# A macaron block on one core: first weights loaded in 112 and 15 rows, and the steps of norms, recurrence and routing placed further apart

## The reference

```
x = x + 0.5 * moe(norm(x))      # 8 experts, 128 -> 512 -> 128, relu, the best 2 gates of a softmax
x = x + rwkv(norm(x))           # time mixing, a recurrence over the tokens, output projection
x = x + 0.5 * moe(norm(x))
x = x + 0.5 * quant_ffn(norm(x))   # int weights, 128 -> 384 -> 128
x = x + attention(norm(x))      # 16 heads of 64, rms norm, all 2048 tokens with each other
x = x + 0.5 * quant_ffn(norm(x))
```

## Time and profile before

| | |
|---|---|
| median of 3 runs | 2288.65 us (2284.3 to 2289.0) |
| profiled execution | 2287.96 us |
| its span, first to last instruction | 2286.2 us |
| mean granted TensorE clock | 0.975 |
| busy in the span | TensorE 87%, VectorE 78%, ScalarE 64%, GpSimd 68% |
| first split product of the first stage | 179.91 us |
| last y_gated of that stage | 633.1 us |

### The profile page before, as it was taken

The page is one execution under the profiler, slowest core; times in us unless marked ns, Lnnn a source line. Parts: engine busy times, 40 slices in busy tenths (PEclk is TensorE's granted clock), DMA queues, the critical chain, the costliest instruction groups (busy, mean ns, idle before and its releaser), DMA issues. The chain is left out here.

```text
span 2286.2 us, 25543 instructions
## 1 busy us (share of the span) xinstructions
PE 1996.4 (87%) x8290; PEld 1421.5 (62%) x8290; DVE 1782.5 (78%) x1964; ACT 1457.9 (64%) x1800; POOL 1543.3 (68%) x767
## 2 busy tenths in 40 slices
PE   1007998899986899999999999999999999999877
PEld 1005776667855576676676766667667667666544
DVE  0005778877655789989989988989998998999785
ACT  0005555554442578877878877878787887887753
POOL 0004233322230589989999998999998998999872
PEclk9999999999987899999999999999999999999987
DMA  1112110112004012312303213123032131230000
GB/s 41 43 47 54 47 33 25 32 38 50 26 14 114 0 40 46 66 20 63 73 13 70 50 36 66 32 52 73 15 69 45 41 67 27 54 71 16 5 1 19
DMA packets 78758, 96.76 MB, mean 42 GB/s; under 512 B 31875, under 2 KB 35379, under 8 KB 78248
## 3 DMA queue, kind: packets, MB, share of 16 engines
q1 hardware_dynamic: 78630, 95.13, 18.2%
HBM read 43.18 MB, written 1.42 MB: 20 GB/s over the span
## 5 line engine op out<-in xcount | busy, mean ns | idle before, releaser
L598 POOL TENSOR_TENSOR p_l<-p_raw,p_h 128x1024 fp32r<-128x1024 f32 x512 | 1240.9, 2452 | 146.0 <-ACT p_h L1246 130.7
L1243 ACT ACTIVATE p_raw<-ps 128x1024 f32<-128x1024 f32 x512 | 566.8, 1107 | 243.1 <-PE ps L870 242.2
L1570 DVE TENSOR_REDUCE m_part<-ps 128x1 f32<-128x1024 f32 x480 | 584.5, 1218 | 126.0 <-PE ps L847 125.0
L1246 ACT ACTIVATE p_h<-ps 128x1024 fp32r<-128x1024 f32 x512 | 523.0, 1021 | 0.0
L869 PE MATMUL ps<-qa,ka 128*128 128x512 f32 x1024 | 445.8, 435 | 2.0 <-ACT m_t L1214 2.0
L870 PE MATMUL ps<-qb,kb 65*128 65x512 f32 x1024 | 409.6, 400 | 0.0
L884 PE MATMUL ps<-p_h,v_hl 128*128 128x512 f32 x1024 | 403.2, 394 | 1.1 <-POOL p_l L598 0.7
L1564 DVE TENSOR_REDUCE l_sum<-p_raw 128x128 f32<-128x1280 f32 x256 | 377.0, 1476 | 0.4
L847 PE MATMUL ps<-ka,qa 128*128 128x512 f32 x960 | 314.5, 409 | 12.2 <-DVE m_part L1570 11.8
L887 PE MATMUL ps<-p_l,v_hl 128*64 128x512 f32 x1024 | 321.6, 395 | 0.0
L1550 DVE TENSOR_REDUCE p_raw<-p_raw 128x128 f32<-128x1024 f32 x256 | 308.9, 1208 | 12.8 <-ACT p_raw L1243 12.8
(11 more groups left out here) (206 smaller groups left out, 2551.7 us busy)
## 6 DMA issues: line engine op xcount, KB each, us to landing
g_bc<-g_scratch SPq DMA_DIRECT2D x64, 256.0 KB, 3.6
xn<-r_scratch SPq DMA_DIRECT2D x59, 256.0 KB, 4.1
qa<-qk_hi SPq DMA_DIRECT2D x112, 128.0 KB, 2.4
ka<-qk_hi SPq DMA_DIRECT2D x56, 128.0 KB, 2.4
kb<-qk_hi SPq DMA_DIRECT2D x56, 128.0 KB, 2.4
ka<-xn SPq DMA_DIRECT2D x28, 128.0 KB, 2.3
qb<-xn SPq DMA_DIRECT2D x28, 128.0 KB, 2.4
ka<-qk_low SPq DMA_DIRECT2D x28, 128.0 KB, 2.7
```

The costliest lines, as they stand in the source:

```text
L598: nc.gpsimd.tensor_tensor(p_l[:, g % 4, :, :], slots(g), p_h[:, g % 4, :, :].bitcast(fp32), ALU.subtract).then_inc(pl_done, 1)
L1243: af(slots(g), s_t, ACT.Exp).then_inc(raw_done, 1)
L1246: af(p_h[:, g % 4, :, :], s_t, ACT.Exp).then_inc(ph_done, 1)
L1570: nc.vector.tensor_reduce(m_part[:, it, half:half + 1], ps[:, 4:6, :].rearrange("p b n -> p (b n)"), AX.X, ALU.max).then_inc(s_max, 1)
```

## The change

The loads of w1 are cut: rows 0 to 126 come as 112 and 15 rows, and row 127 is copied to 128 rows. w2 has its own function, so it can be issued later than w1 of the same part. The first weights are issued right behind x's first chunk, ahead of b1. b_row's transfer stands behind the second part's w1 and not behind the last part. The tables of ticks are new.

```diff
-HEAD_START = 16
+HEAD_START = 18
-ROUTE_AT = (-16, 0, 20, 59, 95, 131, 167, 187)
-RWKV_AT = (40, 76, 112, 148)
-WEIGHTS_AT = (-8, -5, 2, 6, 10, 14, 18, 22)
+ROUTE_AT = (-18, 0, 22, 60, 98, 136, 174, 193)
+RWKV_AT = (40, 78, 116, 154)
+WEIGHTS_AT = (-6, -2, 2, 6, 10, 14, 18, 22)
+MOST = 112
-N_MEAN, N_CEN, N_SQR, N_VAR, N_STD, N_REC, N_SPREAD, N_OUT = 0, 1, 1, 4, 5, 6, 8, 9
+N_MEAN, N_CEN, N_SQR, N_VAR, N_STD, N_REC, N_SPREAD, N_OUT = 0, 1, 2, 5, 6, 7, 10, 11
...
-K_LN, K_INV, K_EA, K_NUM, K_GATE, K_NR, K_NR2, K_OUT, K_PROJECT_OUT, K_ADD = 25, 26, 24, 25, 26, 27, 28, 29, 32, 33
+K_LN, K_INV, K_EA, K_NUM, K_GATE, K_NR, K_NR2, K_OUT, K_PROJECT_OUT, K_ADD = 27, 28, 26, 27, 28, 29, 30, 31, 36, 37
...
-                sp.dma_start(w1_raw[0:C - 1, lo:hi, :], a["w1T"][0:C - 1, lo:hi, :]).then_inc(w1_loaded[i], 16)
-                sp.dma_start(w1_base[0:C - 1, lo:hi, :],
-                             a["w1T"][C - 1:C, lo:hi, :].to_broadcast([C - 1, hi - lo, H0])).then_inc(w1_loaded[i], 16)
+                for rows in (slice(0, MOST), slice(MOST, C - 1)):
+                    sp.dma_start(w1_raw[rows, lo:hi, :], a["w1T"][rows, lo:hi, :]).then_inc(w1_loaded[i], 16)
+                sp.dma_start(w1_base[:, lo:hi, :],
+                             a["w1T"][C - 1:C, lo:hi, :].to_broadcast([C, hi - lo, H0])).then_inc(w1_loaded[i], 16)
...
-                        dve.wait_ge(w1_loaded[[e < hi for _, hi in WEIGHT_PARTS].index(True)], 32)
+                        dve.wait_ge(w1_loaded[[e < hi for _, hi in WEIGHT_PARTS].index(True)], 48)
```

## The result

| kernel | median us | runs | ratio to before [95% interval] |
|---|---|---|---|
| before | 2286.48 | 4 (2282.75 to 2289.0) | |
| changed | 2119.3 | 4 (2114.11 to 2122.26) | 0.9268 [0.9241, 0.9295] |

The forecast was 2116 us, range 2099 to 2136. The profiled execution took 2122.15 us, with a span of 2120.2.

A forecast was written before the change was run, and what follows sets the result against it. The prediction took the start to be bound by one DMA engine of sixteen, moving the 127-row loads at 27 GB/s. From 2288 us, -160.2 for the start and -7, -3, -2 for spacing gave 2116 us, range 2099 to 2136.

The forecast's parts named there:

- The start: Before the first product: recut loads and early b_row bring that product to 19.7 us in place of 179.9.
- The term of -160.2: Time saved before the first product by faster loads and early b_row: 160.2 us.
- All weights near 23: Input loads: the weights of experts 4 to 7 land near 23 us, wanted from tick 10 at 38.
- The routing of the first chunk: After the first product: later h_l and a vanished g_t wait count as even; either could be 3 us.
- The spacing: Expert stage's tick tables: steps further apart remove waits, some 12 us in all, range -12 +12/-15.
- Four such waits, 1.7 each: -7: TensorE's waits for ln_r: the spread three ticks behind N_REC, not two, saves 7 us.
- N_SQR, put at -3: Norm beside the recurrence: N_SQR a tick behind N_CEN removes ScalarE's waits for cen, saving 3 us.
- K_PROJECT_OUT was put at -2: Recurrence's output projection: two ticks further behind the routing's read of the bank, saving 2 us.
- The rest at nothing: Route and recurrence starts moved by 2 to 7 ticks: counted as no gain.
- Rivals 3 and 4: Start loads: 112 rows as slow as 127, 2150 us (4%); base copies hold each other up, 2311 us (1%).
- Rival 1: Expert stage: spacing returns nothing, ln_r waits become h_l waits since VectorE is full; 2128 or 2132 us; 22%.
- Rival 2: Expert stage: spacing returns nearly all its 29 us of TensorE idle time; 2101 us; 13%.

The follow-up runs named there:

- experiment 5: Changed kernel with the loads cut into 113 and 14 rows in place of 112 and 15; 2180.41 us, ratio 0.9538.
- experiment 7: Changed kernel's order and tick tables, but 127 rows in one transfer as before, b_row early; 2262.94 us, ratio 0.9902.
- experiment 2: The new tick tables alone, with the loads and SP's order of the kernel before; 2277.33 us, ratio 0.9971.
- experiment 6: Changed kernel with b_row's transfer behind all weights in SP's order, as before; 2130.88 us, ratio 0.9322.
- experiment 10: Changed kernel with N_SPREAD one tick sooner (9), two ticks behind N_REC as before; 2121.85 us, ratio 0.9278.
- experiment 9: Changed kernel with N_SQR back in N_CEN's tick (1); 2123.37 us, ratio 0.9295.
- experiment 12: Changed kernel with the recurrence's output projection and its add two ticks sooner (34, 35); 2135.17 us, ratio 0.9337.
- experiment 3: Changed kernel with the routing of chunks 3 to 6, norm included, one tick later; 2123.65 us, ratio 0.9298.
- experiment 11: Experiment 8 with the recurrence's third projection and its eviction one tick sooner; 2110.17 us, ratio 0.9219.
- experiment 8: Changed kernel with logits and all later routing steps, turn and rows too, one tick later, head one tick longer; 2108.72 us, ratio 0.9225.

## Why the prediction was right

**The start** came out step by step. Forecast and measured: TensorE starts 6.3 and 6.5; norm ends 15.0 and 15.1; base subtraction ends 16.4 and 16.4; b_row landed near 12, and 8.75 + 2.1 (its landing time in the issues) = 10.9; ScalarE's w_h 17.1 and 17.1; x_l and the first product 19.7, and 19.7 and 19.83. The term of -160.2 is -160.1. Its cause, one engine of sixteen by the row count, is shown by experiment 5 (one row more brings 27 GB/s back) and by experiment 7 (the order without the count gives 14 us against experiment 2); experiment 6 says what the order is worth once the count is right.
The Trainium skill (DMA: Bandwidth & Descriptors, section on why a DMA increments its semaphore by 16) says that a transfer runs on the largest number of engines up to 16 that divides the slowest dimension. The traces agree for 127 rows (share 0.06) and the prime 113 (0.07). For 112 they agree as far as they go: 224 KB landed in 3.6 us (at 27 GB/s they would take 8.5), and the windows of 2 us from 2 to 30 us, in which transfers of 112, 15 and 128 rows are mixed, have shares of 0.61 to 1.12. No run shows 15 rows by themselves.

**All weights near 23** was wrong: 32.2. I had 20 us of transfer at 369 GB/s; the windows of 2 us from 2 to 30 us show 170 to 419. It cost nothing, since no product waited for a weight. Rivals 3 and 4 are out by the same rows.

**The routing of the first chunk** was counted as even, within 3 us. h_l followed the first product by 6.5 us, not 5. But from the first product to the first y_gated it is 18.1 us (19.8 to 37.9), 19.9 before (179.9 to 199.8) and 20.8 with the loads alone: the new loads cost 0.9 there, the tables returned more. "Even" holds.

**The spacing** was mis-sized: forecast -12, measured -5.2, of which -7.8 are idle time of TensorE and +2.5 busy time, with more time at the half clock, a term that the forecast had only for the short stages. The step that failed is "Four such waits, 1.7 each: -7". The waits fell as forecast, 9.3 to 0.6, and experiment 10 shows that this is worth about 1 us: it is the same gap, moved to xn. I had asked what is late behind the spread only for h_l, and not for the next step of the same chain. I had also misread two rows: the 20.6 us in 9 waits for ln_r and the 12.4 in 8 for sqr count a gap at the weight load and again at the matmul. On the matmuls they are 9.3 in 4 and 5.4 in 4. N_SQR, put at -3, came out: its reversal costs 3.5 us of idle time (experiment 9). K_PROJECT_OUT was put at -2, from the 1.8 us of waits; as a term of its own it is wrong, since without it the other moves would have cost 8.5 us more of idle time (experiment 12). "The rest at nothing" was wrong too: the route offset of 20 meets the third projection's eviction of 19 a tick behind it, where it was two ticks, and TensorE waits 5.6 us.

The total came so near (forecast 2116, measured 2119.3) because the start is 160 of the 167 us; for the spacing, the range of -12 +12/-15 would have covered nothing at all as well as twice the forecast.

**Rival 1** named the turning of waits, but into waits for h_l, and these fell from 5.1 to 2.5. It is true in experiment 3, where h_l is what takes over, and for a small part in experiment 11. **Rival 2**, that nearly all of the 29 us come back, found no support in the change, where 7.8 did. But moving a whole chain together (experiment 8) took another 3.5 us of idle time and a tick between eviction and mean (experiment 11) 4.2 more, so VectorE's fullness was not yet the bound.

## What to carry to other kernels

Look at the DMA share of a slow load before its order: 0.06 of sixteen engines was a row count here, and cutting 127 rows into 112 and 15 was worth more than a hundred microseconds, while an order around it was worth 12. Where in-order engines hand one value to and fro in fixed ticks, a tick more at one step is taken from the next step of the chain; move the whole chain with its last consumer, and follow the sum of one engine's idle time, not the wait that went and not the length of the stage alone, which moves with the granted clock too. Set each moved step against every other step that shares its bank.

## What the hardware showed unexpectedly

- A backlog on one DMA engine delays small transfers and SP itself. With 113 rows the 16 KB store of the gates was issued 26 us after g_t was written and took 19.3 us to land; with 127 rows (experiment 7) it took 16.6. The load behind it (g_bc, 256 KB, 5.2 us from issue to landing in the middle of the changed kernel) was waited for 40.5 and 79.4 us.
- The clock of the same stage was not the same in kernels that differ by a tick: some 17 us at the half clock in the changed kernel's stretch, none in experiment 8's, 27 in experiment 12's, with mean clocks over all executions of 0.969 to 0.972, 0.974 to 0.977 and 0.965 to 0.967.
- Small VectorE operations on the routing's 32 columns took 0.19 us, and up to seven times that beside GpSimd's splits of a weight and of x:

```profile
17.25 1.27 POOL L528 TENSOR_TENSOR w_l<-w_raw,w_h 128x512 fp32r<-128x512 f32 x1 [11.91 <-ACT w_h L1100]
...
18.38 0.19 DVE L1406 TENSOR_TENSOR eq<-lg,rt 128x32 f32<-128x32 f32 x1
18.47 1.26 POOL L539 TENSOR_TENSOR x_l<-xn,x_h 127x512 fp32r<-127x512 f32 x1
18.61 1.18 DVE L1407 TENSOR_TENSOR eq<-eq,rank 128x32 f32<-128x32 f32 x1
```

  Four such steps took 1.18, 0.97, 1.32 and 1.19 us; L1406, which began 0.14 us before L528 ended, did not stretch, and L1407 lasted until L539 was through. The same L1407 took 0.19 at 21.72, with GpSimd idle. The single-input step L1409 took 0.19 at 19.82, with GpSimd's next split running. The four make the routing's chain some 4 us longer, more than the 1.5 us by which h_l came later than forecast (6.5, not 5); no run takes them away.
  The Trainium skill (SBUF — State Buffer, section on the two separate sides) says that a VectorE operation with two SBUF inputs and a GpSimd operation that reads SBUF exclude each other on a shared port; the trace agrees, and the price here was up to a whole GpSimd operation for one step.
